# Filling the query and key stacks by three DRAM loads where nine stood, and the maxima's two rows by one transfer where two stood

## The chip, the cores and the metric

The kernel runs on one core of one Trainium2 chip. The metric is the device time of one execution in microseconds. The kernel before took 1169.81 us (median of 3 runs, 1166.87 to 1176.1).

## What is computed

Four transformer blocks run one after the other over a batch of 8 sequences of 256 rows with 256 features; each is conditioned on a vector per sequence, has attention with 16 heads of 16 features, and three of the four have an MLP (256 to 1024 to 256, exact gelu). Layer 1 is causal, layer 2 has no MLP. Cut to one block:

```python
mod = silu(cond) @ Wada + bada                 # shift, scale, gate for attention and MLP
h = layernorm(x) * (1 + scale1) + shift1
q, k, v = split(h @ Wqkv + bqkv)               # 16 heads of 16
attn = softmax(q @ k.T * scale) @ v
x = x + gate1 * (attn @ Wproj + bproj)
h = layernorm(x) * (1 + scale2) + shift2
x = x + gate2 * (gelu(h @ W1 + b1) @ W2 + b2)
```

## The kernel before, in words

**Steps.** The program is a row of 32 steps, one for each layer and sequence (layer 0 sequence 0, 1, ... 7, then layer 1 and so on), software-pipelined. In step g the attention of sequence g runs, with the MLP of the step before (`c`) and the q, k, v products of the step after (`a`). Every engine has its own hand-written order of work in a function `step`, and waits on semaphores for the others. A step with an MLP beside it takes some 35 us, one without (steps 17 to 24, which are those after a step of layer 2, and step 0) some 29 to 31 us.

**Split operands.** The scores must be exact to float32, but TensorE reads float32r here. So q and k are each split in a high and a low part (`q_hi`, `q_lo`, `k_hi`, `k_lo`, each 128 partitions x 2 x 256 floats, 256 KB). ACT writes the high part (`hi_part`), DVE the low one (`lo_part`). A score is the sum of three products, hi*hi, hi*lo and lo*hi, and these are done in one matmul with the three stacked along the contraction: `k_stack` holds, for each of the 32 rows of a pair of heads, three partitions (96 = `KB` in all), with k_hi, k_lo, k_hi; `q_stack` holds q_hi, q_hi, q_lo, with the two heads of a pair in the two halves of the 96 partitions and zeros elsewhere.

**The way through DRAM.** Rows must move to other partitions, so the four parts are stored in a DRAM scratch `qk_dram` (function `spill`, four stores of 256 KB) and read back (function `stack`): q by six loads of 16 partitions x 8 x 256 (three parts, two heads), k by three loads of 32 x 8 x 256. The destination's partitions are every third one. All of this is issued by SP, whose queue holds for each step in this order: the four stores, the nine loads, the load of the gate and bias rows `par_sb` (512 KB, broadcast to 128 partitions), in layer 3 a store of a finished sequence, then the maxima.

**The maxima.** TensorE writes the scores S of a tile of queries in `s_bank` (function `score`, 16 tiles a step), DVE takes the negated row maxima (`score_max`), splits them in high and low parts (`max_split`), TensorE transposes these (`max_turn`), DVE copies them to `max_t` (16 rows x 256: 8 heads high, 8 heads low), and two DMAs (`max_rows`, 8 KB each) put them in partitions 96 and 97 of `q_stack`, under the three parts. This happens twice a step, for heads 0 to 7 (half 0) and 8 to 15 (half 1). Then the transposed scores (`score_t`, contraction 98) come out with the maximum subtracted already, and ACT takes the exponential. In `score_t`, the first pair of a half waits for the DMAs on the semaphore `max_ld`. In steps with an MLP the two DMAs are on SP's queue, in the others on ACT's. Half 0 of step a is moved in step g, half 1 of step g in step g.

**Who waits for what.** `score` of the next step begins with a wait for all nine loads (`stack_ld`). The high and low parts share their memory with the hidden layer, so that ACT's first gelu waits for all four stores (`q_spill`, `k_spill`). Where a step has no MLP, SP waits for `max_ld` before it loads `par_sb`.

## Time and profile before

| | us |
|---|---|
| median of 3 runs (range) | 1169.81 (1166.87 to 1176.1) |
| the profiled execution, its own time | 1167.0 |
| its span, first to last instruction | 1165.2 |
| TensorE matmul busy | 1066.8 (92% of the span) |
| VectorE busy | 836.0 (72%) |
| ScalarE busy | 570.5 (49%) |
| GpSimd busy | 326.6 (28%) |
| DMA queue q1 (SP), share of 16 engines | 33.2% |
| granted TensorE clock, mean | 0.978 of 2.4 GHz |

The profiled execution's own time is 1.8 us over its span, and 2.8 us under the median of the runs. A share of busy time is a mean over stages of different kinds: steps with an MLP keep TensorE at some 97 to 98%, those without at some 85%. In the tables of waits, a line is a group of instructions, what it waited for, the total in us, the number of times and the longest.

### The profile page before, as it was taken

The page shows a single profiled execution, that of the slowest core. Times are in us where ns is not written, and L with a number is a line of the kernel's source. Part 1 is how long each engine was busy: PE and PEld are TensorE (multiplying, and loading weights), DVE is VectorE, ACT ScalarE, POOL GpSimd, SP SyncE. Part 2 cuts the span into 40 slices and gives each one's busy share as a digit, 9 for nine tenths or more (in the row PEclk, how much of TensorE's full clock was granted, in tenths as well). Part 3 has the DMA queues.
Part 4 walks back from the last instruction along what each step waited for, and adds up shares of the span by engine and source line. Part 5 has one row for each costly group of instructions (what it writes and reads, how often), then busy time and mean ns, then how long its engine had stood idle before and what let it go on. Part 6 is the DMA issues. An engine that isn't in the chain of part 4 may idle for free.

```text
span 1165.2 us, 22743 instructions
## 1 busy us (share of the span) xinstructions
PE 1066.8 (92%) x8002; PEld 868.4 (75%) x8002; DVE 836.0 (72%) x2187; ACT 570.5 (49%) x1140; POOL 326.6 (28%) x408
## 2 busy tenths in 40 slices
PE   5789999999998999999999988888888999999987
PEld 4568888788886888888888755555656888788776
DVE  4477777777787877778787676666677777777743
ACT  4244565554553455545446444444445456555451
POOL 3033331233336333212333101111134333113332
PEclk9799999999999999999999998899889999999999
DMA  7732333222343235331233433333352133322300
GB/s 235 241 102 75 110 111 110 69 64 87 110 156 116 61 110 165 111 109 63 69 101 110 137 111 110 102 118 110 93 188 85 56 111 118 120 81 72 110 3 19
DMA packets 103279, 123.26 MB, mean 106 GB/s; under 512 B 9040, under 2 KB 96080, under 8 KB 102288
## 3 DMA queue, kind: packets, MB, share of 16 engines
q1 hardware_dynamic: 102608, 121.73, 33.2%
q8 instruction: 56, 0.92, 0.3%
q10 hardware_dynamic: 576, 0.30, 0.1%
q14 instruction: 39, 0.32, 0.1%
HBM read 85.16 MB, written 35.78 MB: 104 GB/s over the span
## 4 chain that ended last, share of the span: by engine, by line
PE 61%; DVE 13%; DMA 7%; issue 7%; ACT 5%; POOL 4%; SPq 1%; ACTq 0%; POOLq 0%; DVEq 0%
PE dense L1181 8%; PE o_banks L1331 8%; PE dense L1253 8%; PE s_bank L1278 7%; PE dense L1236 7%; DMA q_stack<-max_t 6%; PE st_bank L1315 5%; PE o_banks L1210 4%; DVE neg_max L865 3%; POOL hid_lo L522 3%; PE o_banks L1160 2%; PE o_banks L1339 2%; ACT probs L673 2%; PE o_banks L1196 2%; PE s_bank L1288 2%
## 5 line engine op out<-in xcount | busy, mean ns | idle before, releaser
L673 ACT ACTIVATE probs<-st_bank 128x512 f32<-128x512 f32 (+1 forms) x512 | 264.9, 571 | 167.8 <-PE st_bank L1315 116.6
L865 DVE TENSOR_REDUCE neg_max<-s_bank 128x2 f32<-128x512 f32 x384 | 255.3, 685 | 58.7 <-PE s_bank L1278 55.3
L1278 PE MATMUL s_bank<-k_stack,q_stack 96*128 96x256 f32 (+1 forms) x1024 | 228.7, 315 | 21.8 <-DMA k_stack<-qk_dram 10.3
L1278 PEld LDWEIGHTS s_bank<-k_stack,q_stack 96*128 96x128 f32 x1024 | 167.5, 195 | 63.9 <-DVE neg_max L865 21.6
L522 POOL TENSOR_TENSOR hid_lo<-hid,hid_hi 128x512 fp32r<-128x512 f32 x96 | 125.8, 1320 | 267.4 <-DVE hid_hi L977 267.4
L474 POOL TENSOR_TENSOR veps<-mv,eps_c 128x2 f32<-128x2 f32 x65 | 18.1, 278 | 511.0 <-DVE mv L831 511.0
L1315 PE MATMUL st_bank<-q_stack,k_stack 98*128 98x512 f32 x384 | 146.2, 452 | 14.9 <-DMA q_stack<-max_t 12.2
L661 ACT ACTIVATE hid<-dense,vec 128x256 f32<-128x256 f32 x192 | 80.6, 472 | 110.5 <-PE dense L1236 110.5
L1331 PE MATMUL o_banks<-probs,v_aug 128*32 128x256 f32 (+1 forms) x2048 | 123.8, 384 | 9.5 <-DVE xg L904 5.8
L1181 PE MATMUL dense<-ht,w_sb 128*128 128x256 f32 x512 | 127.7, 389 | 3.9 <-ACT ht L612 1.3
L1236 PE MATMUL dense<-ht,w_hi 128*128 128x256 f32 x384 | 116.4, 303 | 7.4 <-DVE ht_lo L970 6.2
L1253 PE MATMUL dense<-w_hi,hid_hi 128*128 128x256 f32 x384 | 115.2, 300 | 5.1 <-POOL hid_lo L522 5.1
L1181 PEld LDWEIGHTS dense<-ht,w_sb 128*128 128x128 f32 x512 | 96.0, 195 | 17.7 <-issue 5.5
L1253 PE MATMUL dense<-w_lo,hid_hi 128*128 128x256 f32 x384 | 108.3, 282 | 0.0
L1236 PE MATMUL dense<-ht_lo,w_hi 128*128 128x256 f32 x384 | 108.3, 282 | 0.0
L1236 PE MATMUL dense<-ht,w_lo 128*128 128x256 f32 x384 | 108.3, 282 | 0.0
L1253 PE MATMUL dense<-w_hi,hid_lo 128*128 128x256 f32 x384 | 107.9, 281 | 0.0
L1331 PEld LDWEIGHTS o_banks<-probs,v_aug 128*32 128x32 f32 x2048 | 64.0, 113 | 50.9 <-issue 9.5
L1315 PEld LDWEIGHTS st_bank<-q_stack,k_stack 98*128 98x128 f32 x384 | 66.2, 190 | 40.2 <-ACT probs L673 17.8
L860 DVE CUSTOM_DVE_ANT_0 s_bank<-s_bank,mask_q 128x128 f32<-128x128 f32 (+1 forms) x256 | 85.7, 383 | 14.4 <-PE s_bank L1278 13.5
L977 DVE CAST hid_hi<-hid 128x512 fp32r<-128x512 f32 x96 | 75.2, 801 | 18.8 <-ACT hid L661 18.8
L1236 PEld LDWEIGHTS dense<-ht,w_hi 128*128 128x128 f32 x384 | 72.9, 190 | 19.6 <-DVE ht_lo L970 10.3
(136 smaller groups left out, 1889.4 us busy)
## 6 DMA issues: line engine op xcount, KB each, us to landing
q_stack<-qk_dram SPq DMA_DIRECT2D x192, 128.0 KB, 2.9
k_stack<-qk_dram SPq DMA_DIRECT2D x96, 256.0 KB, 4.0
par_sb<-par_dram SPq DMA_DIRECT2D x32, 512.0 KB, 5.1
qk_dram<-q_hi SPq DMA_DIRECT2D x32, 256.0 KB, 2.1
qk_dram<-q_lo SPq DMA_DIRECT2D x32, 256.0 KB, 2.1
qk_dram<-k_hi SPq DMA_DIRECT2D x32, 256.0 KB, 2.2
qk_dram<-k_lo SPq DMA_DIRECT2D x32, 256.0 KB, 2.1
w_sb<-w SPq DMA_DIRECT2D x5, 1024.0 KB, 9.7
```

Source lines behind the costliest of these rows:

```text
L522: nc.gpsimd.tensor_tensor(hid_lo[:, js].bitcast(F32R), hid[:, js], hid_hi[:, js], ALU.subtract).then_inc(hid_lo_sb, 1)
L661: ins = nc.scalar.activation(hid[:, 2 * i + k], src[:, k], ACT.Gelu, bias=col(l, "b1", 2 * i + k))
L673: nc.scalar.activation(probs[p % 4][:, kt, :, q0:N], src, ACT.Exp, scale=SCORE_SCALE[l]).then_inc(p_sb, 1)
L860: ins = nc.vector.tensor_tensor_reduce(out=s, in0=s, in1=mask_q[:, (1 - qt) * P:2 * P], scale=-1.0, scalar=-MASKED, op0=ALU.add, op1=ALU.m ...
L865: nc.vector.tensor_reduce(neg_max[:, qt, 2 * p:2 * p + 2], split3(bank[:]), AX.X, ALU.max, negate=True).then_inc(s_max, 1)
L977: nc.vector.tensor_copy(hid_hi[:, js].bitcast(F32R), hid[:, js]).then_inc(hid_hi_sb, 1)
L1181: ins = mm(dense[bank][:, t * N:(t + 1) * N], w_qkv(a.layer, kt, c0, c0 + P), ht1[:, kt], start=kt == 0, stop=kt == KT - 1)
L1236: ins = mm(dense[(i + 1) % 2][:, k * N:(k + 1) * N], w, h.bitcast(F32R), start=n == 0, stop=n == len(terms) - 1)
L1253: ins = mm(dense[1][:, t * D:(t + 1) * D], h[:, j, t * P:(t + 1) * P].bitcast(F32R), w[l % 2][:, j].bitcast(F32R), start=j == 0 and n == 0 ...
L1278: ins = mm(bank[:, e * N:e * N + k1], q_stack[g.par][0:KB, 2 * p + e, qt * P:(qt + 1) * P].bitcast(F32R), k_stack[g.par][0:KB, p, 0:k1].bi ...
L1315: mm(split3(st_bank[kt][:]), *stacks(g, p, kt, 0), start=True, stop=True).then_inc(st_ps, 1)
L1331: ins = mm(o_bank[i][32 * j:32 * j + 32, q0:N], v_aug[g.par][:, kt, 8 * h + 4 * i + j, :], pr[:, kt, j % 2, q0:N], start=kt == 0, stop=kt ...
```

## The change

The scratch `qk_dram` gets a dimension for the three parts as the stack holds them: for q (hi, hi, lo), for k (hi, lo, hi), so that row r's three parts lie behind each other. `spill` therefore stores the high part twice, six stores of 256 KB for four. `stack` then reads three neighbouring rows as three neighbouring partitions: q by two loads of 48 x 8 x 256, k by one of 96 x 8 x 256. The bytes read are the same, 1.5 MB a step; those stored grow from 1.0 to 1.5 MB. In `max_rows` the two transfers of 8 rows each become one of 16 rows to 2 partitions. The counts in the waits follow (48 for 32 of the stores, 48 for 144 of the loads, 32 for 64 of the maxima); those that only change so are cut here but for two.

```diff
-    qk_dram = nc.dram_tensor("qk_dram", (2, 4, KT, P, N), F32).ap()
+    qk_dram = nc.dram_tensor("qk_dram", (2, 2, KT, P, 3, N), F32).ap()
...
             wait(eng, max_sb, g.count(2, half + 1))
             h0 = half * H // 2
-            for part in range(2):
-                dst = q_stack[g.par][KB + part:KB + part + 1, h0:h0 + H // 2, :]
-                src = max_t[half][part * H // 2:(part + 1) * H // 2, :]
-                eng.dma_start(dst, src).then_inc(max_ld, 16)
+            dst = q_stack[g.par][KB:KM, h0:h0 + H // 2, :]
+            eng.dma_start(dst, max_t[half][:]).then_inc(max_ld, 16)
...
             def spill(a):
-                for part, tile, ready in ((0, q_hi, q_hi_sb), (1, q_lo, q_lo_sb), (2, k_hi, k_hi_sb), (3, k_lo, k_lo_sb)):
-                    wait(sp, ready, a.count(1, 1))
-                    dst = qk_dram[a.par, part].rearrange("t p n -> p t n")
-                    sp.dma_start(dst, tile[:]).then_inc(q_spill if part < 2 else k_spill, 16)
-
-            def rows_of(a, part):
-
-                return qk_dram[a.par, part].rearrange("t (j r) n -> r (t j) n", j=4)
+                for which, hi, hi_sb, lo, lo_sb, spilled in ((0, q_hi, q_hi_sb, q_lo, q_lo_sb, q_spill),
+                                                             (1, k_hi, k_hi_sb, k_lo, k_lo_sb, k_spill)):
+                    dst = qk_dram[a.par, which].rearrange("t p c n -> p t c n")
+                    wait(sp, hi_sb, a.count(1, 1))
+                    for c in (0, 1 + which):
+                        sp.dma_start(dst[:, :, c], hi[:]).then_inc(spilled, 16)
+                    wait(sp, lo_sb, a.count(1, 1))
+                    sp.dma_start(dst[:, :, 2 - which], lo[:]).then_inc(spilled, 16)
 
             def stack(a):
-                wait(sp, q_spill, a.count(32, 32))
-                for quad, part in enumerate((0, 0, 1)):
-                    for e in range(2):
-
-                        r0 = 3 * e * HD + quad
-                        src = rows_of(a, part)[e * HD:(e + 1) * HD]
-                        dst = q_stack[a.par][r0:r0 + 3 * HD - 2:3].rearrange("r (p e) n -> r p e n", e=2)[:, :, e, :]
-                        sp.dma_start(dst, src).then_inc(stack_ld, 16)
-                wait(sp, k_spill, a.count(32, 32))
-                for quad, part in enumerate((2, 3, 2)):
-                    sp.dma_start(k_stack[a.par][quad:quad + KB - 2:3], rows_of(a, part)).then_inc(stack_ld, 16)
+                rows = [qk_dram[a.par, which].rearrange("t (j r) c n -> (r c) (t j) n", j=4) for which in range(2)]
+                wait(sp, q_spill, a.count(48, 48))
+                for e in range(2):
+
+                    half = slice(e * 3 * HD, (e + 1) * 3 * HD)
+                    dst = q_stack[a.par][half].rearrange("r (p e) n -> r p e n", e=2)[:, :, e, :]
+                    sp.dma_start(dst, rows[0][half]).then_inc(stack_ld, 16)
+                wait(sp, k_spill, a.count(48, 48))
+                sp.dma_start(k_stack[a.par][0:KB], rows[1]).then_inc(stack_ld, 16)
...
-                    wait(sp, max_ld, g.count(64, 64))
+                    wait(sp, max_ld, g.count(32, 32))
...
-                        wait(pe, stack_ld, g.count(144, 144))
+                        wait(pe, stack_ld, g.count(48, 48))
```

SP's queue in a step of the loop, from the stores to the load of `par_sb` (a row is a line of the program, the instruction, out<-in with its shape, and the semaphores waited for; xN is N like it in a row). The kernel before:

```order
L352 DMA qk_dram<-q_hi 128x2x256 [waits q_hi_sb]
L352 DMA qk_dram<-q_lo 128x2x256 [waits q_lo_sb]
L352 DMA qk_dram<-k_hi 128x2x256 [waits k_hi_sb]
L352 DMA qk_dram<-k_lo 128x2x256 [waits k_lo_sb]
L255 ISA
L366 DMA q_stack<-qk_dram 16x8x256 [waits q_spill]
L366 DMA q_stack<-qk_dram 16x8x256 x5
L369 DMA k_stack<-qk_dram 32x8x256 [waits k_spill]
L369 DMA k_stack<-qk_dram 32x8x256 x2
L391 ISA [waits par_st]
L391 DMA par_sb<-par_dram 128x1024
```

The same place of SP's queue in the changed kernel:

```order
L353 DMA qk_dram<-q_hi 128x2x256 [waits q_hi_sb]
L353 DMA qk_dram<-q_hi 128x2x256
L355 DMA qk_dram<-q_lo 128x2x256 [waits q_lo_sb]
L353 DMA qk_dram<-k_hi 128x2x256 [waits k_hi_sb]
L353 DMA qk_dram<-k_hi 128x2x256
L355 DMA qk_dram<-k_lo 128x2x256 [waits k_lo_sb]
L256 ISA
L364 DMA q_stack<-qk_dram 48x8x256 [waits q_spill]
L364 DMA q_stack<-qk_dram 48x8x256
L366 DMA k_stack<-qk_dram 96x8x256 [waits k_spill]
L388 ISA [waits par_st]
L388 DMA par_sb<-par_dram 128x1024
```

Each second store of a high part stands between the high part's wait and the low part's; six loads have gone from between the last store and `par_sb`.

ACT's queue in a step without an MLP, around the maxima of half 1. The kernel before:

```order
L673 ACTIVATE probs<-st_bank 128x512 [waits st_ps] x7
L604 ACTIVATE v_aug<-o_banks 128x32x16 [waits o_ps,v_ps]
L302 DMA q_stack<-max_t 1x8x256 [waits max_sb]
L302 DMA q_stack<-max_t 1x8x256
L628 ACTIVATE o_sb<-o_banks 128x512 [waits ot_ps,o_ps]
```

The same place of ACT's queue in the changed kernel:

```order
L670 ACTIVATE probs<-st_bank 128x512 [waits st_ps] x7
L601 ACTIVATE v_aug<-o_banks 128x32x16 [waits o_ps,v_ps]
L301 DMA q_stack<-max_t 2x8x256 [waits max_sb]
L625 ACTIVATE o_sb<-o_banks 128x512 [waits ot_ps,o_ps]
```

The second DMA of the maxima has gone, and nothing else moved. TensorE, VectorE and GpSimd have the same instructions in the same order in both kernels.

## Rows read from the trace of the kernel before

**Rows 1.** The page: the chain that ended last, by line, shares of the span
```profile
PE dense L1181 8%; PE o_banks L1331 8%; PE dense L1253 8%; PE s_bank L1278 7%; PE dense L1236 7%; DMA q_stack<-max_t 6%; PE st_bank L1315 5%; PE o_banks L1210 4%; DVE neg_max L865 3%; POOL hid_lo L522 3%; PE o_banks L1160 2%; PE o_banks L1339 2%; ACT probs L673 2%; PE o_banks L1196 2%; PE s_bank L1288 2%
```

**Rows 2.** Waits of PE in layers 0, 1, 2, 3 (from 80 us), then one of all
```profile
PE dense L1253 <- POOL hid_lo L522: 1.8, 6, 0.4
PE st_bank L1315 <- DMA q_stack<-max_t: 1.8, 3, 1.3
...
PE st_bank L1307 <- DMA q_stack<-max_t: 2.4, 5, 0.9
...
PE st_bank L1315 <- DMA q_stack<-max_t: 5.6, 8, 1.0
...
PE st_bank L1315 <- DMA q_stack<-max_t: 4.8, 5, 1.3
...
PE s_bank L1278 <- DMA k_stack<-qk_dram: 10.3, 6, 8.0
```

**Rows 3.** Chain in a step of layer 3 (start us, us, what), and PE's timeline [idle before]
```profile
942.77 0.70 SPq L302
...
943.51 3.38 DMA q_stack<-max_t
...
946.94 0.73 PE L1315 MATMUL st_bank<-q_stack,k_stack 98*128 98x512 f32 x2 [0.82 <-DMA q_stack<-max_t]
```

**Rows 4.** Timeline of SP's queue in that step: start us, us, issue
```profile
933.89 0.36 SPq L352 DMA_DIRECT2D qk_dram<-k_lo  x1
934.29 3.85 SPq L366 DMA_DIRECT2D q_stack<-qk_dram  x6
938.18 3.00 SPq L369 DMA_DIRECT2D k_stack<-qk_dram  x3
941.29 0.55 SPq L391 DMA_DIRECT2D par_sb<-par_dram  x1
```

**Rows 5.** DMA engines' busy tenths from 934 to 950 us, slices of 0.4 us; bytes moved
```profile
DMA  9498467476675968999158999889820000000000
...
q1 hardware_dynamic: 2608, 2.84, 57.5%
```

**Rows 6.** The chain in a step of layer 1
```profile
591.36 0.70 SPq L302
...
592.10 2.93 DMA q_stack<-max_t
```

**Rows 7.** The page's DMA queues, ACT's: packets, MB, share of 16 engines
```profile
q10 hardware_dynamic: 576, 0.30, 0.1%
```

**Rows 8.** Timelines of PE and ACT and the chain, a step of layer 2
```profile
755.19 0.73 PE L1315 MATMUL st_bank<-q_stack,k_stack 98*128 98x512 f32 x2 [0.74 <-DMA q_stack<-max_t]
755.76 0.60 PE L1339 MATMUL o_banks<-ident,o_sb 128*128 128x128 f32 x4
...
754.51 0.60 ACT L628 ACTIVATE o_sb<-o_banks 128x512 f32<-128x512 f32 x1 [2.31 <-PE o_banks L1331]
...
751.62 3.53 DMA q_stack<-max_t
```

**Rows 9.** The chain at the start
```profile
18.75 2.15 DMA qk_dram<-q_lo
...
26.20 5.43 DMA k_stack<-qk_dram
```

**Rows 10.** Windows of two steps of layer 2 (granted clock third from the end), and their starts in the chain
```profile
708.00:739.00 31.00, 26.82 (x164) 18.40 (x164) 19.77 (x49) 13.89 (x29) 4.88 (x7) 0.89 0.34 104
739.00:768.00 29.00, 24.36 (x165) 17.41 (x166) 19.98 (x49) 13.98 (x29) 4.89 (x7) 1.00 0.37 111
...
708.73 3.69 PE dense L1181 x16
...
739.64 3.69 PE dense L1181 x16
...
768.35 3.69 PE dense L1181 x16
```

More of the change, by code:

```diff
@@ L580, in hi_part @@
             def hi_part(a, which, ps, bank, dst, done, spilled):
-                wait(act, spilled, a.count(32, 0))
+                wait(act, spilled, a.count(48, 0))
                 wait(act, ps, a.count(1, 1))
@@ L655, in gelus @@
                         if a.exists:
-                            wait(act, q_spill, a.count(32, 32))
-                            wait(act, k_spill, a.count(32, 32))
+                            wait(act, q_spill, a.count(48, 48))
+                            wait(act, k_spill, a.count(48, 48))
                     wait(act, w1_ps, c.mlp(4, i + 1))
@@ L880, in max_copy @@
                 wait(dve, max_ps, g.count(2, half + 1))
-                wait(dve, max_ld, g.count(64, 32 * half + 32 - 64))
+                wait(dve, max_ld, g.count(32, 16 * half + 16 - 32))
                 nc.vector.tensor_copy(max_t[half][:], s_bank[half % 2][0:H, 0:N]).then_inc(max_sb, 1)
@@ L885, in lo_part @@
                 l = a.layer
-                wait(dve, spilled, a.count(32, 0))
+                wait(dve, spilled, a.count(48, 0))
                 wait(dve, ready, a.count(1, 1))
@@ L1299, in score_t @@
                     if p == 0:
-                        wait(pe, max_ld, g.count(64, 32))
+                        wait(pe, max_ld, g.count(32, 16))
                     if p == PAIRS // 2:
-                        wait(pe, max_ld, g.count(64, 64))
+                        wait(pe, max_ld, g.count(32, 32))
                     if CAUSAL[g.layer]:
```

## The prediction, made before the changed kernel ran

> **What bounds the kernel now.** I read the page first, for the chain that ended last: some 60% of it is TensorE, spread over all its products, and a single transfer, that of the maxima, stands among them with 6% [rows 1]. A share of the chain is not yet a price, because the engine may work on something else under it. So the second view is the waits of PE, by layer. There the reader is to see how little is really lost: PE stood still for the maxima 1.8 us in layer 0, 2.4 in layer 1, 5.6 in layer 2 and 4.8 in layer 3, 14.6 us in 21 waits; for the stacks it stood still 10.3 us in 6 waits, of which one, at the start, is 8.0 [rows 2]. Everything that the change can win by shorter DMA is in these 24.9 us, save what follows from the clock.
>
> The third view is one such wait from near. In a step of layer 3 SP issues the two transfers one after the other from 942.77, the second lands at 943.51 + 3.38 = 946.89, and PE starts at 946.94 after standing still for 0.82 us; it was free at 946.1 [rows 3]. In a quiet place the same pair takes 0.70 + 0.04 + 2.93 = 3.67 us from the first issue to the landing [rows 6], here it takes 4.12. Why it is late is in SP's queue and the DMA engines: between the last store (933.89) and the load of par_sb (941.29) stand nine loads, 3.85 + 3.00 us of issuing [rows 4], and the engines are busy in eight or nine tenths until slice 29 of 40, which is 945.6 [rows 5]. The transfer of the maxima queues behind par_sb, on the same queue.
>
> **The change part by part, in a step with an MLP.** (1) Stores: two more issues of 0.36 us [rows 4]. The second one of a high part stands where SP waits for the low part anyway, so its issue costs nothing; its 256 KB cost the engines time. 2.84 MB took 57.5% of 16 us, 9.2 us of all engines [rows 5], which is 0.83 us for 256 KB. The last store of k then lands up to 0.8 us later. Before, the loads of k were issued 3.9 us after those of q [rows 4], now they would come at 1.3 us, so they wait for that store: last store issued at 933.89, plus 2.15 us as such a store took at the start [rows 9], plus 0.8, is 936.8. (2) Loads: six q issues of 0.64 us become two, three of k become one. I take 0.64 us for each; the new shapes are not in the trace, and the bounds are 0.6 (a load that moved 16 or 32 partitions took the same) and 1.9 (what is left of the 3.00 us of the three k loads if two took 0.6: an issue that was held up). So par_sb, issued at 941.29 before, is issued at 936.8 + 0.6 = 937.5, with the k load before it; the engines still have the same bytes to move. From 934 on they were busy for 9.2 of 11.6 us; without the gaps and with up to 0.8 us more of stores they end at 934 + 9.2 + 0.8 = 944.0 instead of 945.6. (3) Maxima: one issue for two, 0.74 us off the path [rows 3]. A single one that is not held up would land at 942.77 + 2.93 = 945.70.
>
> In this step PE is free at 946.1 and the maxima land at 945.7, or somewhat later for the reason below. The wait is gone. What is late next is hid_lo: in layer 0, where most steps have no wait for the maxima, PE waits 0.3 us for POOL in each (1.8 us in 6 times) [rows 2], a little later in the same step. So a step gives its wait less 0.3. Steps with an MLP have 1.8 + 2.4 + 4.8 = 9.0 us of waits for maxima and 10.3 - 8.0 = 2.3 us for stacks, in 13 steps: 11.3 - 13 x 0.3 = 7.4 us.
>
> **Layer 2.** Here ACT issues the maxima on its own queue, and the second lands at 751.62 + 3.53 = 755.15 while SP's stack loads fill the engines; PE lost 0.74 us [rows 8]. Without the first issue, and with the stack loads drained earlier, it lands by 754.4, when PE is free. But PE's next work, the transposes of o_sb, started at 755.76, and ACT has o_sb ready at 754.51 + 0.60 = 755.11 [rows 8], so they cannot start before 755.15: 0.6 us won, of 0.74. For eight steps 5.6 - 8 x 0.17 = 4.2 us. ACT's saved issue itself is worth nothing, since ACT then waits 2.31 us for PE.
>
> **The start.** PE waited 8.0 us for k_stack [rows 2], with nothing beside it. The first k store waits do not move. Before: the q store lands at 18.75 + 2.15 = 20.90, nine issues, the last at 26.20, landing at 31.63 [rows 9]. Now: q loads at 20.9 and 21.6; k load after its store, at some 23.3; its 768 KB take 3 x 0.83 = 2.5 us, and with the other 2.2 us of a lone transfer (2.93 - 0.7) and the q bytes ahead it lands at about 28.5. That is 3.0 us won, all on the path. Bounds are 0 (the engines are the limit and the extra stores eat the gain) and 5.3 (all of the removed issues but one, 31.63 - 26.3).
>
> **Sum.** 7.4 + 4.2 + 3.0 = 14.6 us off the profiled execution's own time: 1167.0 - 14.6 = 1152.4. That execution was 2.8 us faster than the median of the runs; I put half of this on top and say 1154.
>
> **What speaks against part (3).** ACT's queue moved 576 packets for 0.30 MB in 36 transfers [rows 7]: 288 of 1 KB, and as many without weight. So I read that each transfer of 8 rows ran on eight engines, one row on each. The new one has 16 rows at its source and 2 partitions at its destination, and how many engines it gets no row shows. At best it is eight or more, and nothing is lost; at worst two, one for each partition, with eight rows one behind the other. By the rate above (0.83 us for 256 rows on 16 engines, 0.052 us a row) eight rows take 0.42 us in place of 0.05, 0.37 us more. I take the worse end: in the step of layer 3 the landing moves from 945.7 to 946.1, just when PE is free, and the sum stands. The Trainium skill (DMA: Bandwidth & Descriptors, "Why a DMA increments its semaphore by 16 and not by 1") says that the number of engines is the largest one, up to 16, that divides the slowest dimension above 1 of both sides. For 8 and 8 that is eight, and the trace agrees with its 288 packets beside the 288 of data; for 16 and 2 it would be two, which leaves the sum and gives the mechanism of the rivals (A) and (C).
>
> **Rivals.** (A) The maxima gain 0.74 - 0.37 us by one issue less on two engines, but the engines' work is what they wait for, and it doesn't end earlier. For: the engines are at eight or nine tenths from the k loads on [rows 5]. Against: in the q phase they were at four to seven tenths, and there is room to move work forward. Then the steps with an MLP give nothing, layer 2 gives 8 x 0.37 = 3.0, the start 3.0: 1161, within 1%. (B) The clock. In layer 2 the step that starts at 739.64 takes 28.7 us, the one at 708.73 takes 30.9, and the granted clock is 1.00 in the first and 0.89 in the second, a part of it at the lower of the two levels, 1.2 GHz [rows 10]; I assume, and no row proves it, that it falls because PE works thinly there, and the waits for the maxima [rows 2] are a part of that. If the shorter wait keeps the clock up in the four such steps, 4 x 2.2 = 8.8 us more go: 1143.6. It can also fall in more of them, since where it falls depends on where the thin stretches lie: three more would be 6.6 us, and 1159. I take it as unchanged. (C) Slower: the extra stores delay everything that is on SP's queue, and the maxima come on two crowded engines. Its place is the landing of half 1 in each of the 31 steps; the pair had 942.77 to 946.1, 3.3 us, before it costs anything. From a landing later than that on it decides. With the backlog ending 0.8 us later than before (946.4) and 0.42 us for eight rows, it lands 0.5 to 0.6 us later than now in 31 steps: 17 us, less the 3 of the start, gives 1181. Against it: six issues have gone from ahead of par_sb. (D) The change doesn't do what it says, for example a load of 96 partitions is issued in pieces of 1.9 us or more: two or three us of the start are lost, and nothing elsewhere, since SP waits for the maxima with its queue empty; 1157.
>
> **How the numbers follow.** The forecast with its neighbour (D) has 0.55, (A) 0.22, (B) upward 0.10 and downward (more stretches at the low clock) 0.05, (C) 0.08. About 1% of 1170, 11.7 us, is what a measurement can tell from no change; faster by more means below 1158.1. The forecast is on that side 9 times in 10, since its terms are bounded by waits that are seen; with (B) upward it makes 0.6. Within 1%: (A), the rest of the forecast and half of the low clock, 0.32. Slower 0.08. The range: upward to just beyond (A), 1165, since (C) holds less than 1 in 10; downward to (B) upward, 1143.
>
> **What would show it.** In the changed kernel's waits, PE behind the maxima should fall from 14.6 us in 21 times to under 4, that behind k_stack from 10.3 to some 6 to 7, all at the start, and hid_lo should rise by 2 to 4 us. On SP's queue par_sb should be issued 3 to 4 us earlier after the last store. ACT's queue should show 288 packets of 1 KB in 18 transfers with 36 (two engines) to 288 others. Wrong would be: a wait for k_spill that brings par_sb back to where it was, maxima that take over 3.3 us from issue to landing, or a granted clock in layer 2 other than 0.89 in half of the steps.

## The result, and the profile after

| | before | after |
|---|---|---|
| median of 6 runs, us (range) | 1172.2 (1166.87 to 1176.1) | 1197.68 (1188.27 to 1200.05) |
| profiled execution, us | 1167.0 | 1188.27 |
| its span | 1165.2 | 1186.5 |
| PE busy, us | 1066.8 | 1073.6 |
| granted clock, mean | 0.978 | 0.970 (0.952 to 0.967 in the five other runs) |
| queue q1, share of 16 engines | 33.2% | 44.1% |

The changed kernel is slower: the ratio is 1.0207, 95% interval 1.0166 to 1.0247. 1154 us was predicted, with 1165 as the upper end. The profiled execution is the fastest of the six, so its trace shows less than the usual loss.

The page of the changed kernel, chain by line, queues and issues (KB each, median us from issue to landing):

```profile
PE dense L1250 10%; PE dense L1178 9%; DMA k_stack<-qk_dram 8%; PE s_bank L1275 8%; DMA q_stack<-max_t 7%; PE o_banks L1328 7%; PE st_bank L1312 6%; PE dense L1233 4%; PE o_banks L1207 4%; DVE neg_max L862 3%; DMA qk_dram<-k_lo 3%; PE o_banks L1157 2%; PE o_banks L1336 2%; ACT probs L670 2%; PE s_bank L1285 2%
...
q1 hardware_dynamic: 116300, 138.50, 44.1%
...
q10 hardware_dynamic: 324, 0.30, 0.1%
...
q_stack<-qk_dram SPq DMA_DIRECT2D x64, 384.0 KB, 5.8
k_stack<-qk_dram SPq DMA_DIRECT2D x32, 768.0 KB, 7.7
...
...
qk_dram<-k_lo SPq DMA_DIRECT2D x32, 256.0 KB, 3.3
```

The same part of the page of the kernel before:

```profile
q_stack<-qk_dram SPq DMA_DIRECT2D x192, 128.0 KB, 2.9
k_stack<-qk_dram SPq DMA_DIRECT2D x96, 256.0 KB, 4.0
...
qk_dram<-k_lo SPq DMA_DIRECT2D x32, 256.0 KB, 2.1
```

Two lines are new in the chain beside [rows 1]: the load of k with 8% and the store of k_lo with 3%. That store takes 3.3 us from its issue to landing where it took 2.1, and the k load has to wait for it.

Waits of PE of the changed kernel, in the windows of layers 0 to 3 (80 to 355, 355 to 640, 640 to 900, from 900 us), then two of all:

```profile
PE s_bank L1275 <- DMA k_stack<-qk_dram: 2.8, 5, 1.1
PE st_bank L1312 <- DMA q_stack<-max_t: 0.9, 3, 0.4
...
PE s_bank L1275 <- DMA k_stack<-qk_dram: 6.7, 6, 1.7
...
PE st_bank L1304 <- DMA q_stack<-max_t: 0.4, 1, 0.4
...
PE st_bank L1312 <- DMA q_stack<-max_t: 18.3, 8, 2.5
...
PE st_bank L1312 <- DMA q_stack<-max_t: 2.7, 3, 1.0
...
PE s_bank L1275 <- DMA k_stack<-qk_dram: 2.1, 3, 1.0
...
PE st_bank L1312 <- DMA q_stack<-max_t: 22.4, 15, 2.5
PE s_bank L1275 <- DMA k_stack<-qk_dram: 19.2, 15, 7.5
```

Beside [rows 2] the reader sees three things. In the layers with an MLP the waits for the maxima fell, from 9.0 to 0.9 + 0.4 + 2.7 = 4.0 us. There PE now waits for k_stack instead: 2.8 + 6.7 + 2.1 = 11.6 us, where it was 2.3. And in layer 2 the waits for the maxima grew from 5.6 to 18.3 us, in the same eight steps. In all, maxima and stacks grew from 24.9 to 22.4 + 0.4 + 19.2 = 42.0 us, by 17.1; PE busy grew by 6.8 with the same products, which is the clock. The two make 23.9 us beside 21.3 of longer span; the waits for hid_lo gave 2.1 of the difference back (5.1 to 3.0).

**A step of layer 2.** SP's timeline, first before, then after (start us, us, issue):

```profile
742.57 0.36 SPq L352 DMA_DIRECT2D qk_dram<-q_hi  x1
...
745.27 0.36 SPq L352 DMA_DIRECT2D qk_dram<-k_lo  x1
745.72 3.80 SPq L366 DMA_DIRECT2D q_stack<-qk_dram  x6
749.56 1.91 SPq L369 DMA_DIRECT2D k_stack<-qk_dram  x3
755.17 0.35 SPq L391 DMA_DIRECT2D par_sb<-par_dram  x1
```

```profile
756.87 0.89 SPq L353 DMA_DIRECT2D qk_dram<-q_hi  x2
...
759.63 0.72 SPq L355 DMA_DIRECT2D qk_dram<-k_lo  x1
760.63 1.27 SPq L364 DMA_DIRECT2D q_stack<-qk_dram  x2
763.23 0.30 SPq L366 DMA_DIRECT2D k_stack<-qk_dram  x1
771.05 0.36 SPq L388 DMA_DIRECT2D par_sb<-par_dram  x1
```

Here SP issues `par_sb` when the maxima have landed, so the rows give the whole period. Loads begin 3.15 us after the first store's issue before, 3.76 after; the maxima are in 9.45 and 10.42 us later. The sum is 12.6 and 14.2 us. Over the eight such steps the means are 12.64 and 14.27: 1.6 us each, 13 us in all, and the wait grew by 12.7. The chain of the same step of the changed kernel shows the transfer itself, 5.76 us where [rows 8] has 3.53:

```profile
765.26 5.76 DMA q_stack<-max_t
```

DMA engines of the changed kernel from 756 us, slices of 0.4 us (busy tenths, GB/s):

```profile
DMA  0000599999999999969999999999999999600000
GB/s 0 0 0 0 187 335 320 371 318 364 323 356 330 356 333 220 174 187 364 202 161 161 172 274 212 251 238 220 243 212 230 243 238 200 138 13 0 0 0 0
```

The engines are full from the first store to 770. While they store they move 318 to 371 GB/s; while they load, mostly 160 to 250. The maxima, issued by ACT at 765.26, land when the loads are over.

**A step of layer 3** of the changed kernel. SP's timeline, then the chain, then PE's timeline [idle before]:

```profile
955.55 0.46 SPq L355 DMA_DIRECT2D qk_dram<-k_lo  x1
...
958.69 0.30 SPq L366 DMA_DIRECT2D k_stack<-qk_dram  x1
959.10 0.48 SPq L388 DMA_DIRECT2D par_sb<-par_dram  x1
```

```profile
958.69 9.16 DMA k_stack<-qk_dram
```

```profile
967.89 0.50 PE L1275 MATMUL s_bank<-k_stack,q_stack 96*128 96x256 f32 x2 [1.04 <-DMA k_stack<-qk_dram]
```

`par_sb` follows the last store by 3.55 us, where it was 7.4 [rows 4]: it did come forward. But it only joins the k load, which takes 9.16 us, and PE stands still 1.04 us for it.

### The profile page after: what moved, and what is told of

Its sections match the earlier page's. It is cut to its first block, busy times and chain, and to the rows that moved or that the text cites. A ratio compares the mean times of both kernels' runs of the same rounds, so it can differ in the third digit from the quotient of the medians.

```text
span 1186.5 us, 22551 instructions
## 1 busy us (share of the span) xinstructions
PE 1073.6 (90%) x8002; PEld 876.1 (74%) x8002; DVE 833.8 (70%) x2187; ACT 569.8 (48%) x1140; POOL 323.4 (27%) x408
## 3 DMA queue, kind: packets, MB, share of 16 engines
q1 hardware_dynamic: 116300, 138.50, 44.1%
## 4 chain that ended last, share of the span: by engine, by line
PE 58%; DMA 19%; DVE 12%; ACT 5%; issue 4%; POOL 2%; SPq 1%; POOLq 0%; DVEq 0%; ACTq 0%
PE dense L1250 10%; PE dense L1178 9%; DMA k_stack<-qk_dram 8%; PE s_bank L1275 8%; DMA q_stack<-max_t 7%; PE o_banks L1328 7%; PE st_bank L1312 6%; PE dense L1233 4%; PE o_banks L1207 4%; DVE neg_max L862 3%; DMA qk_dram<-k_lo 3%; PE o_banks L1157 2%; PE o_banks L1336 2%; ACT probs L670 2%; PE s_bank L1285 2%
## 5 line engine op out<-in xcount | busy, mean ns | idle before, releaser
L1275 PE MATMUL s_bank<-k_stack,q_stack 96*128 96x256 f32 (+1 forms) x1024 | 232.2, 319 | 29.5 <-DMA k_stack<-qk_dram 19.2
L1275 PEld LDWEIGHTS s_bank<-k_stack,q_stack 96*128 96x128 f32 x1024 | 170.5, 199 | 72.8 <-DMA k_stack<-qk_dram 23.6
L1312 PE MATMUL st_bank<-q_stack,k_stack 98*128 98x512 f32 x384 | 149.6, 464 | 24.1 <-DMA q_stack<-max_t 22.4
L1312 PEld LDWEIGHTS st_bank<-q_stack,k_stack 98*128 98x128 f32 x384 | 68.6, 198 | 47.4 <-DMA q_stack<-max_t 25.2
L857 DVE CUSTOM_DVE_ANT_0 s_bank<-s_bank,mask_q 128x128 f32<-128x128 f32 (+1 forms) x256 | 85.7, 383 | 19.2 <-PE s_bank L1275 18.4
L1233 PEld LDWEIGHTS dense<-ht,w_hi 128*128 128x128 f32 x384 | 72.9, 190 | 19.7 <-DVE ht_lo L967 10.4
L974 DVE CAST hid_hi<-hid 128x512 fp32r<-128x512 f32 x96 | 71.0, 757 | 18.7 <-ACT hid L658 18.7
```

What stands on the lines that cost most here:

```text
L857: ins = nc.vector.tensor_tensor_reduce(out=s, in0=s, in1=mask_q[:, (1 - qt) * P:2 * P], scale=-1.0, scalar=-MASKED, op0=ALU.add, op1=ALU.m ...
L974: nc.vector.tensor_copy(hid_hi[:, js].bitcast(F32R), hid[:, js]).then_inc(hid_hi_sb, 1)
L1233: ins = mm(dense[(i + 1) % 2][:, k * N:(k + 1) * N], w, h.bitcast(F32R), start=n == 0, stop=n == len(terms) - 1)
L1275: ins = mm(bank[:, e * N:e * N + k1], q_stack[g.par][0:KB, 2 * p + e, qt * P:(qt + 1) * P].bitcast(F32R), k_stack[g.par][0:KB, p, 0:k1].bi ...
L1312: mm(split3(st_bank[kt][:]), *stacks(g, p, kt, 0), start=True, stop=True).then_inc(st_ps, 1)
```

## The experiments

Ratios are to the kernel before on the same chip, with a 95% interval. The first four take the change apart. Waits are read from one execution of each kernel, the profiled one.

**Only the merged maxima.** Edit to the kernel before:

```diff
-            for part in range(2):
-                dst = q_stack[g.par][KB + part:KB + part + 1, h0:h0 + H // 2, :]
-                src = max_t[half][part * H // 2:(part + 1) * H // 2, :]
-                eng.dma_start(dst, src).then_inc(max_ld, 16)
+            dst = q_stack[g.par][KB:KM, h0:h0 + H // 2, :]
+            eng.dma_start(dst, max_t[half][:]).then_inc(max_ld, 16)
```

> The kernel before with only the maxima's two transfers made one (the scratch as before). Theory L (the loss comes from the large loads and the extra stores, and the one transfer of the maxima is only hurt by what stands ahead of it): with the old loads the one transfer lands some 0.3 to 0.7 us earlier than the pair, PE's waits for the maxima fall from 14.6 us to 4 to 9 us, and the kernel takes 0.2 to 0.8% less than before. Theory M (one transfer of 16 rows to 2 partitions runs on two engines, and this is what costs in layer 2): the waits for the maxima in the eight steps without an MLP grow from 5.6 us to 10 or more, and the kernel is 0 to 1% slower than before. ACT's queue should show 324 packets, as in the changed kernel, in both cases.

Measured: 1168.68 us, ratio 0.9971 (0.9935 to 1.0006). PE waits for the maxima 8.9 us at L1313 and 0.4 at L1305, where it was 14.6 in all, and for k_stack 12.1, where it was 10.3. Theory L fits: in layer 2 the waits for the maxima are 4.0 us, not 10 or more. The merged transfer does no harm; the 0.3% are not clear of zero.

**Only the scratch, six stores and three loads**, that is the changed kernel with the edit above taken back:

> The changed kernel with the maxima in two transfers of 8 rows again (six stores, three loads). Theory L: about as slow as the changed kernel, 1.5 to 2.5% over before; waits for k_stack some 19 us, for the maxima in layer 2 some 15 us or more since both transfers stand beside the 768 KB load. Theory M: most of the loss in layer 2 is gone, waits for the maxima there 6 to 9 us, and the kernel is 0.5 to 1.2% over before.

Measured: 1205.05 us, ratio 1.0274 (1.0226 to 1.0323), clock 0.953, waits for the maxima 25.4 us at L1314 and 2.2 at L1306, for k_stack 18.7. The whole loss is here, as theory L had it, and somewhat more of it than L allowed. The changed kernel, with the merged maxima, waits for them 22.8 us and not 27.6; its ratio of 1.0207 is 0.7% lower, but the two intervals overlap.

**Six stores, nine loads.** New scratch, but loads of every third row:

```diff
-                    half = slice(e * 3 * HD, (e + 1) * 3 * HD)
-                    dst = q_stack[a.par][half].rearrange("r (p e) n -> r p e n", e=2)[:, :, e, :]
-                    sp.dma_start(dst, rows[0][half]).then_inc(stack_ld, 16)
+                        r0 = 3 * e * HD + c
+                        dst = q_stack[a.par][r0:r0 + 3 * HD - 2:3].rearrange("r (p e) n -> r p e n", e=2)[:, :, e, :]
+                        sp.dma_start(dst, rows[0][r0:r0 + 3 * HD - 2:3]).then_inc(stack_ld, 16)
...
-                sp.dma_start(k_stack[a.par][0:KB], rows[1]).then_inc(stack_ld, 16)
+                for c in range(3):
+                    sp.dma_start(k_stack[a.par][c:c + KB - 2:3], rows[1][c:c + KB - 2:3]).then_inc(stack_ld, 16)
```

> The kernel before with six stores in the new scratch, but nine loads as before (every third partition, now every third row of the scratch) and two transfers of the maxima. Theory L1 (the three large loads run at a lower rate, 1 KB packets of 75 to 140 ns, because of their shape): the loads' packets are back at 50 to 60 ns, q1's share is some 36 to 38%, the time 0 to 0.7% over before, the cost of 0.5 MB more of stores alone. Theory L2 (the extra stores cost, by their bytes and by delaying the wait for the stores): 1 to 2% over before. Theory L3 (the order of the rows in the new scratch makes the reads slow, however they are cut): packets of the loads stay at 75 ns and more, share 42 to 45%, 1.5% or more over before.

Measured: 1182.98 us, ratio 1.011 (1.0064 to 1.0157), clock 0.980 in the profiled execution and 0.967 to 0.978 in the others. Share of q1 38.8%, the k loads land after 4.1 us. Its timeline of SP in layer 2:

```profile
749.99 0.88 SPq L355 DMA_DIRECT2D qk_dram<-q_hi  x2
...
753.71 3.84 SPq L367 DMA_DIRECT2D q_stack<-qk_dram  x6
...
763.23 0.35 SPq L392 DMA_DIRECT2D par_sb<-par_dram  x1
```

The loads begin 3.72 us after the first store and take 9.52, nearly as before (9.45). In the mean of the eight steps of layer 2 they begin 0.7 us later than before, and the whole ends 0.5 us later. So the two stores alone push everything back and cost 1.1%. This is the price of L2; the loads themselves are about as quick as L1 said.

**Three loads, four stores.** Two transfers for the maxima; the second copies of the high parts are stored in the first two steps only, so that from the third on a part of each stack is stale (the bytes and the work are the same):

```diff
-                    for c in (0, 1 + which):
+                    for c in (0, 1 + which) if a.reg is None and a.off < 2 else (0,):
```

> The changed kernel with two transfers of the maxima, and without the second store of the high parts from step 2 on (the loads then read old values for one of the three parts, so the scores are not those of the reference): four stores, three loads. Theory L1 or L3: the loads stay slow (last load lands 7 us or more after its issue), q1's share near 40%, 0.7 to 1.7% over before. Theory L2: as fast as before or faster, down to 1% under it, since three loads replace nine and nothing else is added.

Measured: 1172.74 us, ratio 1.0018 (0.9993 to 1.0043), clock 0.978; k_stack cost PE 9.9 us, much as before [rows 2]. SP in layer 2:

```profile
746.92 0.38 SPq L361 DMA_DIRECT2D qk_dram<-q_hi  x1
...
750.08 0.98 SPq L372 DMA_DIRECT2D q_stack<-qk_dram  x2
751.80 0.30 SPq L374 DMA_DIRECT2D k_stack<-qk_dram  x1
759.74 0.36 SPq L396 DMA_DIRECT2D par_sb<-par_dram  x1
```

This is what the loads were worth without the stores: nothing. SP has issued its last load 7.6 us before all has landed, and the end did not come forward: 9.66 us from the first load to the end, where nine loads took 9.45, and 9.83 against 9.42 in the mean of the eight steps. The time is that of L2, but the loads are slow as L1 and L3 had it: the k load lands after 8.2 us, and q1's share is 40.2%, for the same bytes as the 33.2% of the kernel before. The same can be read within the step. Two windows of the kernel before, in which q loads and then k loads move, and the same two of this kernel; the last two figures are the share of the DMA engines (it adds up the packets' times, and those overlap enough to pass 1) and GB/s:

```profile
747.60:751.20 3.60, 3.29 (x19) 2.56 (x18) 2.18 (x6) 1.65 (x4) 0.00 (x0) 1.00 0.66 195
751.20:754.00 2.80, 1.97 (x31) 1.22 (x33) 2.17 (x7) 1.01 (x3) 0.43 (x1) 1.00 1.01 273
...
752.00:755.00 3.00, 2.69 (x16) 2.05 (x15) 1.97 (x6) 1.09 (x3) 0.00 (x0) 1.00 1.08 216
755.00:758.40 3.40, 2.57 (x34) 1.69 (x35) 2.38 (x8) 1.57 (x3) 0.39 (x2) 1.00 1.10 238
```

Before, the q loads left the engines a third of their time free. They moved at about the pace at which SP issued them: six of 128 KB in 3.80 us would be 207 GB/s (an estimate from SP's row of that step). With large loads nothing is left free, and the rate is hardly higher; in the k phase it is lower, 238 for 273. So one limit took the place of another, of nearly the same size. Why large loads take more of the engines' time for a byte, no run shows.

**The parts side by side**, from the profiled executions (waits of PE in us, the maxima from 60 us on; both = six stores and three loads, with two transfers of the maxima):

| | maxima, layer 2 | maxima, other layers | k_stack, start | k_stack, others | PE busy |
|---|---|---|---|---|---|
| before | 5.6 | 9.0 | 8.0 | 2.3 | 1066.8 |
| large loads alone | 8.7 | 5.3 | 6.9 | 3.0 | 1070.2 |
| six stores alone | 8.5 | 10.3 | 7.2 | 11.2 | 1067.0 |
| both | 18.8 | 8.8 | 7.4 | 11.3 | 1089.4 |
| both and merged maxima (the changed kernel) | 18.3 | 4.0 | 7.5 | 11.6 | 1073.6 |

The new wait for k_stack is the stores' alone. The zero of the large loads is a gain in the layers with an MLP and a loss in layer 2. And the fall of the maxima's waits from 9.0 to 4.0 us in the changed kernel needs the merged transfer: with two transfers 8.8 are left.

**Par_sb behind the maxima, in the kernel before** (steps with an MLP):

```diff
                 sp.wait_ge(par_st, 16 * (g.layer + 1))
+                if mlp:
+                    max_rows(sp, g, 1)
                 src = par_dram[g.layer].rearrange("b r d -> b (r d)")[bass.ds(g.seq, 1) if g.reg is not None else slice(g.seq, g.seq + 1)]
...
-                if mlp:
-                    max_rows(sp, g, 1)
```

> The kernel before, with the load of par_sb (and in layer 3 the store of the output) issued after the maxima of half 1 in the steps with an MLP, in place of ahead of them. Theory Q (the maxima queue behind par_sb's 512 KB on SP's queue): PE's waits for the maxima in layers 0, 1 and 3 fall from 9.0 us to under 2, the pair lands within 3.1 us, and the time falls by 0.3 to 0.8%. Theory B (the maxima wait for the whole backlog, the stack loads above all): those waits stay above 6 us, and the time is within 0.3% of before. A new wait for par_sb itself at GpSimd's addend would show as POOL waiting for DMA par_sb.

Measured: 1160.93 us, ratio 0.9937 (0.9909 to 0.9965).

```profile
PE dense L1253 <- POOL hid_lo L522: 9.4, 25, 0.7
...
PE st_bank L1315 <- DMA q_stack<-max_t: 5.8, 7, 1.0
```

The waits for the maxima in MLP steps are gone (the 5.8 us are layer 2's), and hid_lo rose by 4.3 us, as the prediction had it for the step that comes late next. With the merged maxima on top:

> The same with the maxima in one transfer too (old scratch, four stores, nine loads). Theory Q: nearly no wait for the maxima in the steps with an MLP, some 3 to 4.5 us left in layer 2, 0.5 to 1.2% faster than before. Theory B: as the kernel with the one transfer alone, 0.3% faster, within the noise of that.

Measured: 1163.05 us, ratio 0.9919 (0.9893 to 0.9946). Theory Q holds in both. Both versions beat both kernels; the order of the queue was worth what the number of transfers was not.

**The same order in the changed kernel:**

> The changed kernel with par_sb (and the output store) issued behind the maxima of half 1 in steps with an MLP. Theory P (in steps with an MLP the maxima queue behind par_sb, as in the kernel before, and the rest of the loss is layer 2 and k_stack): the waits for the maxima in the MLP steps, 4.0 us, go to near 0, those of layer 2 stay at 18, and the time is 0.4 to 0.8% under that of the changed kernel, 1188 to 1193 us, still 1.3 to 1.7% slower than before. Theory Q (the transfer of par_sb is what fills the DMA engines, and the order on the queue is what cost 2%): the time comes back to within 0.5% of before.

Measured: 1195.92 us, ratio 1.0215 (1.0188 to 1.0243), the same as the changed kernel's 1.0207: neither theory's time. The waits did what P said: maxima and k_stack came to 18.2 + 14.4 = 32.6 us, where it was 42.0; layer 2's maxima are 17.8 of them, those of the other layers 0.4. But PE was busy 1090.3 us in that execution, at a clock of 0.956. So what the waits gave, the clock may have taken; the execution is the slowest of its four and that of the changed kernel the fastest of its six, and how much of the difference is the edit's isn't shown.

**Q's halves swapped**, to see whether the slow stretch of the loads belongs to a half (`for e in (1, 0)`):

> The changed kernel with its two q loads issued in the other order (partitions 48 to 95 first). In the changed kernel the stretch in which the second q load moves is the slowest, 140 to 165 GB/s. If it is the place (rows or partitions 48 to 95) that is slow, the slow stretch comes first now, ahead of the other q load; if it is the order (whatever comes second, with the k load beginning behind it), the slow stretch stays second. The time stays within 1% of the changed kernel's in both cases.

Measured, one run: 1208.54 us, clock 0.955. DMA engines from 772 us, slices of 0.4 us, in a step of layer 2 whose q loads are issued at 776.15 and whose `par_sb` at 786.65:

```profile
GB/s 0 0 0 238 343 325 358 330 351 328 351 338 346 330 195 195 210 312 346 261 241 195 138 146 133 136 146 159 225 248 230 233 246 197 72 5 0 0 0 205
```

A stretch of 133 to 159 GB/s starts 4.7 us after the first q load; in the changed kernel one of 161 to 172 starts 3.4 us after it. These are single steps of one execution each. It moved and grew with the order, while the whole took 10.5 us for 10.4. The slow stretch did not come first, as it would if partitions 48 to 95 were slow in themselves; more isn't told apart by this.

**Nine loads of neighbouring rows**, in the changed kernel, to neighbouring partitions (16 for q, 32 for k):

```diff
-                    half = slice(e * 3 * HD, (e + 1) * 3 * HD)
-                    dst = q_stack[a.par][half].rearrange("r (p e) n -> r p e n", e=2)[:, :, e, :]
-                    sp.dma_start(dst, rows[0][half]).then_inc(stack_ld, 16)
+                    for c in range(3):
+                        third = slice((3 * e + c) * HD, (3 * e + c + 1) * HD)
+                        dst = q_stack[a.par][third].rearrange("r (p e) n -> r p e n", e=2)[:, :, e, :]
+                        sp.dma_start(dst, rows[0][third]).then_inc(stack_ld, 16)
...
-                sp.dma_start(k_stack[a.par][0:KB], rows[1]).then_inc(stack_ld, 16)
+                for c in range(3):
+                    third = slice(c * 2 * HD, (c + 1) * 2 * HD)
+                    sp.dma_start(k_stack[a.par][third], rows[1][third]).then_inc(stack_ld, 16)
```

> The changed kernel (six stores, one transfer of the maxima) with its stacks filled by nine loads again, but each of neighbouring rows to neighbouring partitions (16 rows for q, 32 for k). Theory R (a load is slow because each engine moves three or six whole rows of it in a row, with all its packets queued at once): packets take 50 to 60 ns as in the kernel with nine loads of every third row, a q load lands in 3 us or so, a k load in some 4, q1's share is 38 to 39%. Theory S (neighbouring partitions or rows at one time are what is slow): packets stay at 75 ns and over, q1's share at 42% or more, and a q load of 128 KB takes over 3.5 us.

Measured, one run: 1297.23 us. A q load takes 4.9 us to landing, a k load 7.7, and q1's share is 46.5%: theory S. The time was far outside what I had in mind, so the destinations were changed alone, **in the kernel before**:

```diff
-                        r0 = 3 * e * HD + quad
+                        r0 = (2 * quad + e) * HD
                         src = rows_of(a, part)[e * HD:(e + 1) * HD]
-                        dst = q_stack[a.par][r0:r0 + 3 * HD - 2:3].rearrange("r (p e) n -> r p e n", e=2)[:, :, e, :]
+                        dst = q_stack[a.par][r0:r0 + HD].rearrange("r (p e) n -> r p e n", e=2)[:, :, e, :]
...
-                    sp.dma_start(k_stack[a.par][quad:quad + KB - 2:3], rows_of(a, part)).then_inc(stack_ld, 16)
+                    sp.dma_start(k_stack[a.par][2 * quad * HD:2 * (quad + 1) * HD], rows_of(a, part)).then_inc(stack_ld, 16)
```

> The kernel before, with its scratch, its four stores and its nine loads of the same source rows; only the destinations differ: each load fills 16 (q) or 32 (k) partitions that lie beside each other instead of every third one. The same products are added in another order of the rows. Theory N (the destination partitions made the nine neighbouring loads slow): the q loads take about 4.9 us to landing and the k loads about 7.7, as they did with the new scratch, against 2.9 and 4.1 before, and the kernel is 5 to 9% slower, 1230 to 1275 us, with waits for k_stack of 30 us or more. Theory S (the source rows of the new scratch, 3 KB apart, or the extra stores made them slow): the loads take 2.9 and 4.1 us as before and the time is within 0.5% of before. By the Trainium skill (SBUF, the section on the DMA port swizzle) 16 neighbouring partitions reach only a few of the 16 ports, which speaks for N.

Measured, two runs: 1252.41 us, ratio 1.0704 (1.0661 to 1.0747): theory N. PE waited 37.7 us for k_stack and 36.9 for the maxima. Its page, issues:

```profile
q_stack<-qk_dram SPq DMA_DIRECT2D x192, 128.0 KB, 4.5
k_stack<-qk_dram SPq DMA_DIRECT2D x96, 256.0 KB, 7.1
```

The same bytes from the same rows in as many loads, only beside each other in SBUF, take 4.5 and 7.1 us for 2.9 and 4.0. The Trainium skill (SBUF — State Buffer, "Door 1: The DMA port swizzle (why [64,N] ≈ [32,N])") says that the port of a partition follows from some bits of its number, four neighbours sharing one: 16 neighbours reach 4 ports of 16. The runs agree in direction; the number of ports no run shows. By the same rule every third of the first 48 partitions and all 48 of them reach the same 8, so by it the change's large loads are no worse than those of before. The time of three loads with four stores agrees (1.0018); that they fill more of the engines' time (40.2% for 33.2%) the rule leaves open.

**One large load at a time.** I then read that in each kernel with the one load of k, `par_sb` in layer 2 follows that load's issue by 7.6 to 8.5 us, and made a theory of it. First k in three loads:

> The changed kernel with k_stack filled by three loads of every third row, as before, and q_stack by the two large ones. Theory K (what ends last is the one load of k: in layer 2 it landed 7.6 to 8.4 us after its issue in every one of the kernels that have it, whether the q loads began 1.7 or 2.6 us ahead of it, and its issue has to wait for the last store of k, which six stores bring 1.5 us later): the loads end about 9.3 us after the first q load instead of 10.4, the waits for the maxima in layer 2 fall from 18.3 to about 10 us, and the time is 1.0 to 1.5% under that of the changed kernel, 1180 to 1188 us. Rival R (the engines' work on 1.5 MB is what takes 10.4 us, in any cut, or the two q loads are the slow ones): no gain, 1193 to 1202 us.

Measured: 1196.71 us, ratio 1.0213 (1.0159 to 1.0266). Then q in six:

> The changed kernel with q_stack filled by six loads of every third row, as before, and k_stack by the one large load. Theory K (the one load of k takes 7.8 us from its issue): it is issued behind six q issues, some 5 us after the last store's issue instead of 3.7, so in layer 2 the maxima land 1 us later than in the changed kernel, waits for them there rise from 18.3 to about 26 us, and the time is 1205 to 1215 us. Rival R (the large q loads are the slow ones): the time falls to 1180 to 1188 us.

Measured: 1192.14 us, ratio 1.0184 (1.0126 to 1.0242). Theory K is wrong in both; the first lies in R's range, the second in neither. SP in layer 2, k in three, then q in six:

```profile
765.14 1.29 SPq L364 DMA_DIRECT2D q_stack<-qk_dram  x2
...
775.59 0.37 SPq L389 DMA_DIRECT2D par_sb<-par_dram  x1
```

```profile
760.78 3.82 SPq L365 DMA_DIRECT2D q_stack<-qk_dram  x6
...
771.01 0.35 SPq L389 DMA_DIRECT2D par_sb<-par_dram  x1
```

It is 10.45 and 10.23 us from the first load to the end, whichever of the two is large, beside 10.42 with both and 9.52 with neither. The means of the eight steps say the same: 10.43 and 10.30, beside 10.41 and 9.19. The 7.8 us were only the rest of that period. R, as I wrote it (in any cut), is wrong too, since nine loads after six stores took 9.2 to 9.5.

## Why the prediction was wrong

**The step that failed: (2), in which the engines have "the same bytes to move" and end at 944.0 instead of 945.6.** I took 0.83 us for 256 KB, 315 GB/s, from a stretch that mixed stores and loads [rows 5], and used it for loads, and for loads of a new shape. The stores of the changed kernel do run at 318 to 371 GB/s. The loads do not: with four stores the 1.5 MB of a step take 9.42 us from first issue to the maxima's landing in nine loads and 9.83 in three (means of layer 2). The "room at four to seven tenths" that I read in the q phase was there, but moving the issues forward won nothing, because a large load takes more of the engines' time for the same bytes: 216 to 238 GB/s with full engines, where nine loads reached 195 at two thirds of their time and then 273. With SP's issues out of the way the end did not come earlier, and the time was 1.0018 of before. At the start there is little beside it. The chain of the changed kernel:

```profile
20.36 3.32 DMA qk_dram<-k_lo
...
23.69 7.74 DMA k_stack<-qk_dram
```

I had the k load issued at 23.3 (it was 23.69), and its landing at 28.5, with 3 x 0.83 us for its bytes. It landed at 31.43, against 31.63 before: 0.2 us of the 3.0. Even these are not a gain, since the start differs by more between executions: from the first q load to the last landing it was 10.27 us in the changed kernel and 10.65 in the kernel before, but 9.8, 9.9 and 10.7 in three other versions with the same stores and loads as before. The two bounds of this term held, and I took the middle where the lower end (0, "the engines are the limit and the extra stores eat the gain") was right. So rival (A) had the outcome right, that the backlog doesn't end earlier; its reason, that the engines' work stays the same, was not right either.

**Part (1), the stores.** "Up to 0.8 us" was nearly right as a size (the loads begin 0.6 to 0.7 us later), but I let the shorter loads pay for it. Since they pay nothing, the stores cost 1.1% by themselves. That is rival (C)'s mechanism. Its place was half right: in the layers with an MLP the waits for the maxima fell (9.0 to 4.0 us, but only with the merged transfer), and what came late was a wait that I had let go to nothing, k_stack, 2.3 to 11.6 us. In layer 2, where I forecast a gain of 4.2 us, 12.7 were lost.

**What exceeds the sum of the parts.** Stores alone 1.1%, large loads alone 0.2%, both 2.7%; half of the loss is in neither part. In layer 2 it can be read in the mean over the eight steps, first store's issue to `par_sb`: 12.64 before, 13.08 with large loads, 13.10 with six stores, 14.27 in the changed kernel (14.33 with two transfers of the maxima), 0.7 more than the sum. In the table above the larger share of the excess is PE's busy time, that is the clock: 22.6 us over before with both, 0.2 with the stores and 3.4 with the large loads. I had no rival with this in it. The last two runs show that either large load is enough for the 0.7 us; why is open. That no run isolates it is a gap: the stores' packets still under way when the first large load starts are one candidate, untested.

**Part (3), the maxima.** Right in its mechanism. 324 packets are 288 of data and 36 others: two engines in each of 18 transfers, the worse of the two ends. The Trainium skill's rule named in the prediction (DMA: Bandwidth & Descriptors, "Why a DMA increments its semaphore by 16 and not by 1") gives two engines as well. PE's waits for the maxima fell by 5 us with it, both alone (14.6 to 9.3) and within the change (27.6 to 22.8); in the times, 0.9971 alone and 1.0274 to 1.0207 within the change, neither difference is clear of the intervals.

**Layer 2, and (B), the clock.** I left the clock unchanged. It fell. Two windows of the changed kernel (granted clock third from the end), one at the higher level and the one behind it at the lower, 1.2 GHz:

```profile
682.00:709.00 27.00, 20.01 (x128) 14.16 (x125) 16.17 (x42) 9.88 (x21) 0.95 (x2) 1.00 0.49 121
709.00:719.00 10.00, 9.65 (x52) 6.07 (x51) 6.05 (x15) 4.03 (x9) 3.55 (x5) 0.50 0.13 51
```

PE stood idle for 7.0 of 27 us, then the clock was low for 10. The changed kernel has five such low stretches in layer 2, 41 us in all (14, 10, 3, 10 and 3), where the kernel before has four of 7 us, 27. 14 us more at half speed cost up to 7, about the 6.8 of PE's busy time; 7 us more of low clock lie ahead of layer 2. The medians lie 25.5 us apart and the profiled executions 21.3, and the five other executions had a lower clock yet. Six stores with nine loads, whose waits are 37.3 us, had a clock of 0.967 to 0.980 in their eight executions; all with a large load behind six stores had 0.952 to 0.970. That thin stretches bring the clock down is supported by this, not shown by itself.

**The size.** (C) gave 1181 and had a chance of 0.08. The sum of the measured terms is 1167.0 + 17.1 + 6.8 - 2.1 = 1188.8, beside 1188.27. That sum is bookkeeping of two executions, not a forecast. What misled the chances: both (A) and (C) hung on one number, the rate of loads, and part of it could have been read before. From the first q load (745.72) to the maxima's landing at 755.15 [rows 8] the 1.5 MB of loads take 9.4 us, and I had used it nowhere. It would not have settled the question, since SP was issuing in 5.7 of the 9.4 us, and the change takes most of that away; the rate of the new shape stood in no row, and wanted a run of the loads alone.

## What to carry to other kernels

Before cutting the number of transfers, read from one step how long the same bytes take from the first issue to the last landing, loads by themselves, and run the new shape alone: engines that stand free in a third of their time are no promise, since larger loads may fill them without ending earlier (0.66 to 1.08 of their time, 195 to 216 GB/s). Stores added ahead of the loads cost 1.1% here by themselves. Look also at the order on the queue: moving a 512 KB load behind two transfers of 8 KB gave 0.6% in the kernel before, where three loads for nine, bought with two more stores, lost 2%; in the changed kernel the same order gave nothing. And when a load's destination may be chosen, spread its partitions: beside each other they cost 7.0%.

## What was not expected of the hardware

- Destination partitions alone change the speed of loads: 16 neighbours 4.5 us and 32 neighbours 7.1 us to landing, against 2.9 and 4.0 for every third one, and 7.0% of the time.
- An issue's cost does not go by its bytes: on SP's queue a load of 96 partitions took 0.30 us (768 KB), where three of 32 at every third partition took 1.91, and six of 16 took 3.80. With neighbouring partitions the three took 1.42 and the six 2.81.
- The same bytes took 33.2% of the engines' time in nine loads and 40.2% in three, in the same total time.
- Writes to DRAM, from 128 partitions, ran at 318 to 371 GB/s, the loads behind them, of 1 KB rows to 48 or 96 partitions, mostly at 160 to 250. It is not loads as such: in the same step of the kernel before, `par_sb`, 4 KB rows to 128 partitions, reached 379 in a slice of 0.4 us. Whether the rows, the partitions or the direction make the difference, no run separates.
- Six stores with large loads behind them cost 0.7 us in a step of layer 2 more than the sum of the two edits, and either of the two kinds (q or k) was enough for it.
